# Own rows added when an expert's output leaves PSUM, gated biases from TensorE, and 18 read-back buffers in place of 8

## The reference, cut to what matters

```
x = x + gnn(xn) + mix(xn)                       # "x1" in the kernel, one row of 256 per node
scores = layernorm(attention sums over edges)   # 4 scores per node
w = softmax of the two best scores              # so the gates g[0..3] of a node add up to 1
out = 0
for e in range(4):
    hh  = gelu(layernorm(x) @ W1[e] + b1[e])
    out = out + g[e] * (hh @ W2[e] + b2[e])
return x + out
```

## Time and profile before

| what | value |
|---|---|
| median of 3 runs | 4428.18 us |
| the profiled execution | 4423.44 us |
| its span | 4421.7 us |
| busy in the span: PE / DVE / POOL / ACT | 73% / 47% / 66% / 19% |
| mean granted TensorE clock | 0.887 |

### The profile page before, as it was taken

One profiled execution on the slowest core, in us unless ns is written; L12 is line 12 of the kernel. 1 busy time (PEld: TensorE's weight loads), 2 busy tenths in 40 slices (PEclk: granted clock), 3 DMA queues, 4 the chain that ended last, 5 costly groups with the idle time before them and its releaser, 6 DMA issues. The chain is left out here.

```text
span 4421.7 us, 47627 instructions
## 1 busy us (share of the span) xinstructions
PE 3239.6 (73%) x12938; PEld 2172.7 (49%) x12938; DVE 2066.9 (47%) x4749; ACT 831.6 (19%) x2082; POOL 2897.5 (66%) x3009
## 2 busy tenths in 40 slices
PE   0118999999997777777777739999999999994000
PEld 0105656665654555555555426666666666663000
DVE  8885565555654454444444411132323223233677
ACT  4301222222220111111111111222222222221000
POOL 1617777777777777776676767777777777754210
PEclk6559999999999989998898869999999999997555
DMA  6205555555555566665565422222222222223766
GB/s 202 100 22 136 137 137 137 137 137 137 137 137 135 150 164 181 163 163 157 157 168 159 109 62 59 66 73 66 73 66 73 66 66 73 66 66 105 220 210 219
DMA packets 378974, 540.08 MB, mean 122 GB/s; under 512 B 117914, under 2 KB 295418, under 8 KB 378743
## 3 DMA queue, kind: packets, MB, share of 16 engines
q0 software_dynamic: 119136, 234.44, 23.4%
q1 hardware_dynamic: 259735, 304.59, 21.2%
HBM read 392.03 MB, written 146.74 MB: 122 GB/s over the span
## 5 line engine op out<-in xcount | busy, mean ns | idle before, releaser
L792 POOL DMA_INDIRECT rows<-xn_rows,gsrc x1664 | 1577.9, 948 | 579.0 <-issue 494.4
L1262 POOL DMA_INDIRECT nb<-route_rows,idx x1024 | 1011.6, 988 | 319.6 <-issue 305.4
L1017 PE MATMUL PS<-rows,oh 128*128 128x257 f32 x3328 | 826.9, 397 | 132.4 <-DMA rows<-xn_rows,gsrc 131.4
L1017 PEld LDWEIGHTS PS<-rows,oh 128*128 128x128 f32 x3328 | 624.3, 195 | 260.6 <-DMA rows<-xn_rows,gsrc 160.8
L1587 PE MATMUL PS<-arena,hid 128*125 128x256 f32 x3200 | 697.5, 380 | 20.9 <-ACT hid L1552 20.9
L1579 PE MATMUL PS<-x2g,arena 128*128 128x500 f32 x1600 | 679.0, 585 | 44.5 <-DMA x2g<-x_turned 42.3
L1587 PEld LDWEIGHTS PS<-arena,hid 128*125 128x125 f32 x3200 | 598.5, 188 | 129.6 <-issue 33.1
L1526 DVE TENSOR_TENSOR y_sb<-PS,b_b 125x512 f32<-125x512 f32 x200 | 128.7, 685 | 1058.8 <-PE PS L1587 1058.6
L1579 PEld LDWEIGHTS PS<-x2g,arena 128*128 128x128 f32 x1600 | 305.5, 191 | 403.9 <-issue 357.7
L1088 PE MATMUL PS<-own_w,p_t 128*125 128x512 f32 x400 | 259.7, 736 | 249.9 <-issue 131.3
L1552 ACT ACTIVATE hid<-PS,b_sb 128x500 f32<-128x500 f32 x400 | 270.8, 677 | 616.1 <-PE PS L1579 616.1
(11 more groups left out here) (300 smaller groups left out, 3355.6 us busy)
## 6 DMA issues: line engine op xcount, KB each, us to landing
y_rows<-y_sb SPq DMA_DIRECT2D x100, 512.0 KB, 2.7
arena<-y_rows SPq DMA_DIRECT2D x100, 512.0 KB, 4.9
rows<-xn_rows,gsrc POOLq DMA_INDIRECT x1664
nb<-route_rows,idx POOLq DMA_INDIRECT x1024
sum_rows<-kept SPq DMA_DIRECT2D x104, 128.5 KB
x_rows<-x SPq DMA_DIRECT2D x100, 128.0 KB, 4.1
hid<-x_rows SPq DMA_DIRECT2D x100, 128.0 KB, 8.4
m_in<-sum_rows SPq DMA_DIRECT2D x100, 125.5 KB
```

Source lines behind the costliest of these rows:

```text
L792: pool.indirect_dma_start(out=rows[w][h][:, q, 0:D], out_offset=None, in_=xn_rows, in_offset=bass.IndirectOffsetOnAxis(ap=gsrc[:, s * HU + ...
L1017: last = mm(SUM[:, 0:D + 1], oh[w][h][:, q, :], rows[w][h][:, q, :], start=h == 0 and q == 0, stop=h == 1 and q == HU - 1)
L1262: pool.indirect_dma_start(out=nb[b % NBUF][:, c, :], out_offset=None, in_=route_rows, in_offset=bass.IndirectOffsetOnAxis(ap=idx[:, b * W ...
```

## The change

1. `y_sb` gets the own rows x1 in place of the biases. SP loads x1 for a whole group into `x1_own` (one 500 KB DMA a group, ahead of the group's inputs), and DVE adds it to each of the four outputs as it copies them from PSUM. The gates add up to 1, so the gated sum of the outputs then holds x1 once.
2. The gated biases come from TensorE in the combine phase. POOL clears `b2_steps` (in the memory of `nb`) once the last batch is used, and SP puts b2 into it 20 times, as a block diagonal. After each `weigh(k)` PE turns the gates of 20 tiles (`GT`), ACT copies them to `gate_t`, and PE makes one product of 125 x 256 per tile into one of four PSUM banks (`GB`). The first operation of `combine(t)` takes it in place of x1.
3. The load of 128 KB of x1 rows per tile in the combine phase is gone.
4. There are 18 read-back buffers: four in `ad`, eight in `arena`, six in `hid`. SP starts the first eight loads at tile 97 of the expert phase, the other ten when all `y_rows` are stored.
5. `load_group` now runs at the last tile of a group, not at the first, because `x1_own` is read until there.
6. Some semaphores are merged into shared ones.

The core of the diff:

```diff
-YR = 8
+YR = 18
-            b1_sb, b2_b = one("b1_sb", [P, 16]), one("b2_b", [NP, NE * D])
+            b1_sb, x1_own = one("b1_sb", [P, 16]), two("x1_own", [NP, 4, D])
-            nb = [one(f"nb{q}", [P, W, ROW]) for q in range(NBUF)]
+            nb_all = one("nb_all", [P, NBUF * W * ROW])
+            nb = [nb_all[:, q * W * ROW:(q + 1) * W * ROW].rearrange("p (c r) -> p c r", c=W) for q in range(NBUF)]
+            b2_steps = nb_all[0:NE * FT, 0:FT * D]
+            gate_t = one("gate_t", [NE * FT, NP])
-            y_in = [arena[:, q * NE * D:(q + 1) * NE * D] for q in range(YR)]
-            x1_in = [hid[:].rearrange("p c n -> p (c n)")[:, q * D:(q + 1) * D] for q in range(YR)]
+            in_tiles = lambda a, n: [a[:, q * NE * D:(q + 1) * NE * D] for q in range(n)]
+            y_in = in_tiles(ad[:].rearrange("p f h -> p (f h)"), 4) + in_tiles(arena, 8) + in_tiles(hid[:].rearrange("p c n -> p (c n)"), 6)
+            GT, GB = PS[2], PS[4:8]
...
                 def load_group(g):
                     u = g % 2
                     if g >= 2:
                         sp.wait_ge(s_hp, (g - 1) * 16)
+                    sp.dma_start(x1_own[u][:], x1_rows[4 * g:4 * g + 4, 0:NP, :].rearrange("t p f -> p t f")).then_inc(s_x2l[u], 16)
...
-                    if t % 4 == 0 and t // 4 + 2 < NG:
+                    if t % 4 == 3 and t // 4 + 2 < NG:
                         load_group(t // 4 + 2)
-                    sp.dma_start(y_in[q], y_rows[t]).then_inc(s_yl[q], 16)
-                    sp.dma_start(x1_in[q], x1_rows[t]).then_inc(s_yl[q], 16)
+                    sp.dma_start(y_in[q], y_rows[t]).then_inc(s_yl[q // 3], 16)
+                    if t == NT - 4:
+                        sp.wait_ge(s_fe, 3)
+                        for k in range(FT):
+                            sp.dma_start(b2_steps[NE * k:NE * (k + 1), k * D:(k + 1) * D], b2).then_inc(s_pl, 16)
+                    if t == NT - 3:
+                        sp.wait_ge(s_ends, 1)
+                        sp.wait_ge(s_hp, NG * 16)
+                        for u in range(2):
+                            sp.wait_ge(s_ys[u], 16 * (NT // 2 - 2))
+                        for k in range(8):
+                            final_loads(k)
...
+                pool.wait_ge(s_nbf, NB)
+                nc.gpsimd.memset(b2_steps, 0.0).then_inc(s_fe, 1)
...
                 def combine(t):
                     q = t % YR
-                    dve.wait_ge(s_yl[q], (t // YR + 1) * 32)
+                    dve.wait_ge(s_yl[q // 3], t // YR * 48 + 16 * min(3, NT - t // 3 * 3))
+                    dve.wait_ge(s_gb, t + 1)
...
-                                                      in1=acc[t % AR][:] if e else x1_in[q][0:NP, :], op0=ALU.mult, op1=ALU.add)
+                                                      in1=acc[t % AR][:] if e else GB[t % 4][0:NP, 0:D], op0=ALU.mult, op1=ALU.add)
+                        if e == 0:
+                            last.then_inc(s_gbd, 1)
...
                     for half in range(2):
-                        last = v.tensor_tensor(y_sb[t % 2][0:NP, half * 512:half * 512 + 512], Y[t % 2][half][0:NP, :],
-                                               b2_b[:, half * 512:half * 512 + 512], ALU.add)
+                        last = v.tensor_tensor(pair(y_sb[t % 2][0:NP, half * 512:half * 512 + 512]), pair(Y[t % 2][half][0:NP, :]),
+                                               x1_own[t // 4 % 2][:, t % 4:t % 4 + 1, :].broadcast_to([NP, 2, D]), ALU.add)
...
+                    act.wait_ge(s_turned, k + 3)
+                    a(gate_t[:], GT[0:NE * FT, 0:NP], ACT.Copy).then_inc(s_exps, 1)
...
+                pe.wait_ge(s_yc, NT)
+                pe.wait_ge(s_pl, 16 * (FT + 4))
+                for k in range(FG):
+                    pe.wait_ge(s_gates, k + 1)
+                    nc.tensor.transpose(GT[0:NE * FT, 0:NP], gate[:, k * FT:(k + 1) * FT, :].rearrange("p t e -> p (t e)"),
+                                        ident[0:NP, 0:NP]).then_inc(s_turned, 1)
+                    pe.wait_ge(s_exps, k + 3)
+                    for j in range(FT):
+                        t = k * FT + j
+                        if t >= 4:
+                            pe.wait_ge(s_gbd, t - 3)
+                        mm(GB[t % 4][0:NP, 0:D], gate_t[:], b2_steps[:, j * D:(j + 1) * D], start=True, stop=True).then_inc(s_gb, 1)
```

More of the change, by code:

```diff
@@ L1160, in build @@
             s_ends = ev("s_ends")
-            s_endt = ev("s_endt")
+            s_turned = ev("s_turned")
             s_endc = ev("s_endc")
-            s_endd = ev("s_endd")
-            s_ende = ev("s_ende")
+            s_diffs = ev("s_diffs")
+            s_exps = ev("s_exps")
             s_fx = ev("s_fx")
-            s_back = ev("s_back")
             s_fix = ev("s_fix")
             s_fixl = ev("s_fixl")
-            s_fixd = ev("s_fixd")
-            s_fixe = ev("s_fixe")
             s_fixed = ev("s_fixed")
@@ L1187, in build @@
             s_ys = [ev(f"s_ys{u}") for u in range(2)]
-            s_yl = [ev(f"s_yl{q}") for q in range(YR)]
+            s_yl = [ev(f"s_yl{q}") for q in range(YR // 3)]
             s_acc = ev("s_acc")
+            s_gates = ev("s_gates")
+            s_gb = ev("s_gb")
+            s_gbd = ev("s_gbd")
             s_out = [ev(f"s_out{q}") for q in range(AR)]
@@ L1197, in _, with final_loads @@
             def _(sp):
-                for to, of in ((b1_sb[:], b1), (b2_b[:], row_of(b2.rearrange("e f -> (e f)"), NE * D)), (bg[:], row_of(b_gat, 16)),
+                for to, of in ((b1_sb[:], b1), (bg[:], row_of(b_gat, 16)),
                                (lg[:], row_of(ln_g, 16)), (lb[:], row_of(ln_b, 16))):
                     sp.dma_start(to, of).then_inc(s_pl, 16)
+                def final_loads(t):
+                    q = t % YR
+                    if t % FT == 0:
+                        k = t // FT
+                        if k >= 2:
+                            sp.wait_ge(s_mrg, k - 1)
+                        sp.dma_start(own[k % 2][:], route_rows[t * NP:(t + FT) * NP, :].rearrange("(t p) c -> p t c", p=NP)).then_inc(s_own, 16)
+                    if t >= YR:
+                        sp.wait_ge(s_acc, t - YR + 1)
+                    sp.dma_start(y_in[q], y_rows[t]).then_inc(s_yl[q // 3], 16)
                 def load_group(g):
@@ L1237, in _ @@
                     sp.wait_ge(s_ys[u], 16 * NT // 2)
-                for t in range(YR):
+                for t in range(8, YR):
                     final_loads(t)
@@ L1369, in over_lanes @@
                 def over_lanes():
-                    dve.wait_ge(s_endt, 1)
+                    dve.wait_ge(s_turned, 1)
                     v.tensor_copy(endt[:], HP[0][0:20, :].rearrange("p (k n) -> p k n", k=4)).then_inc(s_endc, 1)
@@ L1385, in over_lanes @@
                     v.drain()
-                    v.tensor_scalar(dc[:], dc[:], 0.0, None, ALU.min).then_inc(s_endd, 1)
+                    v.tensor_scalar(dc[:], dc[:], 0.0, None, ALU.min).then_inc(s_diffs, 1)
                 def lane_sums():
-                    dve.wait_ge(s_ende, 1)
+                    dve.wait_ge(s_exps, 1)
                     v.tensor_tensor(dc[:, 0, :], dc[:, 0, :], endt[:, 2, :], ALU.mult)
@@ L1395, in first_maxima @@
                 def first_maxima():
-                    dve.wait_ge(s_back, 1)
+                    dve.wait_ge(s_turned, 2)
                     v.tensor_copy(back[:], HP[1][:, 0:40].rearrange("p (k c) -> p k c", k=2))
@@ L1411, in first_maxima @@
                     v.drain()
-                    v.tensor_tensor(d4[:], z4[:, 0:2, :], z4[:, 2:3, :].broadcast_to([P, 2, RH]), ALU.subtract).then_inc(s_fixd, 1)
+                    v.tensor_tensor(d4[:], z4[:, 0:2, :], z4[:, 2:3, :].broadcast_to([P, 2, RH]), ALU.subtract).then_inc(s_diffs, 1)
                 def first_records():
-                    dve.wait_ge(s_fixe, 1)
+                    dve.wait_ge(s_exps, 2)
                     f5 = fix[:, 0:20].rearrange("p (h e) -> p h e", e=5)
@@ L1500, in weigh @@
                     v.drain()
-                    v.tensor_tensor(gate[:, k * FT:(k + 1) * FT, :], sx[:], along(m4[:], 4), ALU.mult)
+                    v.tensor_tensor(gate[:, k * FT:(k + 1) * FT, :], sx[:], along(m4[:], 4), ALU.mult).then_inc(s_gates, 1)
                     v.drain()
@@ L1518, in _ @@
                 v.drain()
-                dve.wait_ge(s_pl, 5 * 16)
+                dve.wait_ge(s_pl, 4 * 16)
                 dve.wait_ge(s_fe, 2)
@@ L1545, in _ @@
                 a = nc.scalar.activation
-                act.wait_ge(s_pl, 5 * 16)
+                act.wait_ge(s_pl, 4 * 16)
                 for g in range(NG):
@@ L1557, in _ @@
                     if g == LAST // 4:
[L1558 to L1561, removed]
+                        act.wait_ge(s_diffs, 1)
+                        a(dc[:], dc[:], ACT.Exp).then_inc(s_exps, 1)
+                act.wait_ge(s_diffs, 2)
+                a(d4[:], d4[:], ACT.Exp).then_inc(s_exps, 1)
```

(6 more changed lines are left out.)

12 lines of the change are left out of this document (3 added, 9 removed).

## The result

The changed kernel takes 4485.52 us (median of 4, 4471.0 to 4487.98) against 4423.69 us for the kernel before in the same rounds. The ratio is 1.0141, with a 95% interval of 1.0123 to 1.0158. That lies outside the predicted range of 4382 to 4436 us. The profiled execution has a span of 4482.6 us.

The account below looks back on a forecast made before the run. PE and POOL were taken to end the expert phase side by side, late stores to stall DVE in the combine phase; -29.5 - 5 + 10.5 + 2.8 + 1.5 = -19.7 from 4423.4 gave 4403.7 us, range 4382 to 4436.

Parts of the forecast that it names:

- x1 in the expert phase: Expert phase: 500 KB more per group, unseen by PE but perhaps felt by POOL's gathers; +1.5 us, bounds 0 and +55.
- Rival C: Expert phase: each of 23 x1 loads makes one gather 2.4 us longer, POOL ends 55 us later; 4457 us, chance 0.10.
- The sign that I named for it: Last batch of the expert phase: a DVE wait for gathers longer than 1 us.
- The x1 loads leave the combine phase: Combine phase: less traffic per tile shrinks 54 short store waits from 36 to 6.5 us; -29.5 us.
- Rival B: Combine phase: short store waits are latency, not bandwidth, so nothing returns; 4438 us, chance 0.15.
- 18 buffers move the own loads: Combine phase: `own` load moves from a block's 13th combine to its third, four long waits 20 us, not 25; -5 us.
- Gated biases: Combine phase: after each of five weighs the first combine waits 2.1 us for PE, ACT, PE; +10.5 us, bounds +7 and +20.
- One operand from PSUM: DVE operations with a PSUM operand take 484 ns against 482 without; 0 us, bounds for this and the PSUM copy -1 and +3.
- The early loads: First eight loads at tile 97: 4 MB in flight when POOL's scatter lands; +2.8 us, bounds 0 and +6.
- b2 loads, POOL's clearing, the stage's start: Twenty b2 issues between stores of tiles 96 and 97, clearing while POOL idles, `b2_b` replaced by `x1_own` at start; each 0.

Follow-up runs that it names:

- disturbed chips: Chips where the kernel before takes some 5850 us; there, 9 read-back buffers against 18, both with eight gathers in flight, gave a combine phase of 376.5 us beside 371.
- mends: Kernel before, without the change, given eight gathers in flight and its stores and own loads cut in 112 and 13 rows: 4374.17 us, ratio 0.9888.

## Why the prediction was wrong, point by point

- **x1 in the expert phase: +1.5 us. This step failed.** It was +86 us to the first weigh (1437.2 to 1523.2), of which the scatter is 3.7. I took the price from gathers beside the inputs' load, whose own duration stays at 0.94 us, and never asked how long a gather may take to land: not over 5.0 us. I read POOL as one that never rests, all its 265.7 us "issue", and passed over the row of 21 waits for landings. Only two of these stand within 5 us of an input load's start; the others come 17 us and more after it, many right behind a long gather of 3.3 us, where the chain has its landings of 4.94 us. So the room was small, and how small beside the input load the profile doesn't say. Nor did I ask how long the new load lasts. I priced it by bytes, and its 125 rows make it run at a quarter of the rate.
- **Rival C had the place, not the mechanism.** It put the loss on POOL's path with a chance of 0.10, and priced it by a gather's duration at 55 us. No gather got longer; POOL waited for landings, 93.4 us. It read the absence of a long gather as evidence against, which it was not. The sign that I named for it did show: DVE's wait for gathers at the last batch is 26.7 us.
- **The x1 loads leave the combine phase, -29.5.** The tiles between the blocks' starts and the long waits take 28.6 us less, so the size held, but by luck: over DVE's 2.08 us each they lost 42.4 us before and 13.8 after (by the starts of the combines in the two timelines), where I had 36 and 6.5. The steady period is 2.30 us and not 2.20. The reason given for the 2.20 was wrong: my rate of 289 KB/us was an average over engines of which five carried the store and were full, and eleven had less to carry. Rival B, latency, is false: the period fell by 0.35 us with the x1 loads gone, and split stores bring it to DVE's 2.09 us.
- **18 buffers move the own loads, -5.** Wrong in sign, and this is nearly all that parts the phase's -16.7 us from the -24 of my terms. The four long waits are 4.97, 9.26, 8.24 and 4.54 us, 27.0 in place of 25. I took SP to be held nearer to 4.72 than to 10.21 us; it was held 7.34, 11.42, 10.77 and 6.83 us, against 10.0 to 10.2 before. Why the middle two are no shorter is open. What the number of buffers does in the steady part by itself no run shows; 18 in place of 9 gave 6 to 7 us of the whole phase, on the disturbed chips.
- **Gated biases, +10.5.** Measured 10.9 us in five waits, 2.2 the longest. Right; no table load, and no wait on PE in mid-block.
- **One operand from PSUM, 0.** Right, 0.48 us in both.
- **The early loads, +2.8.** The scatter took 5.90 in place of 2.19 us, and 1.1 us net with the last gather. The mechanism was right and the bound held; what the last gather gives back I had left out.
- **b2 loads, POOL's clearing, the stage's start, 0.** The clearing took 4.4 us beside nothing that waits, and no wait stands on the b2 loads. Right.

With the loss of 86 us in place of 4.3 the sum would have been 4423.4 - 16.7 + 86 = 4493, against 4484 measured by this execution; the 8.4 us between are the earlier start of its stage.

## What to carry to other kernels

Before adding a DMA beside a chain of small transfers, read how long those take to land and how much time their number in flight covers. A few short waits for landings are the sign that nothing is left, however idle the DMA engines look. Look at the row count of every DMA next: here 125 rows of a 128-row tile cost a factor of three to four in rate, and neither loading 128 nor cutting 112 + 13 cost anything that a run shows. And try a change's mends on the kernel before as well: here they took it to 0.9888 by themselves, and the change added nothing to that.

## What the runs showed of the hardware that was not expected

- A 500 KB load on 125 rows, once the transfers beside it are done, runs at 93 to 107 GB/s and a DMA share of 0.3, while a 512 KB store on 128 rows reaches 350 to 390 GB/s.
- Beside such a load and the input loads, another queue's gathers land after about 8 us, and once after 9.6. Twelve KB more on 128 rows cut the longest wait from 5.2 to 1.8 us.
- SP is held 6.8 to 11.4 us by a load of 2500 rows of 112 bytes on 125 partitions in the combine phase, and 3.1 to 5.4 us by the same rows cut into 112 and 13 partitions.
- On two of the chips the kernel before took about 5850 us in place of 4420, with a granted clock near 0.8. The cause is open.
